# Rewriting the order of work at the end of an attention phase: last softmax first, smaller norm groups

## The reference, cut to what matters

```python
def _L3_gnn_ref(H, W_lin, W_val, a, W_out, A0, src, dst):
    Xq = (H @ W_lin.T).reshape(bt, n, h, dh)
    Xv = (H @ W_val.T).reshape(bt, n, h, dh)
    e = jnp.einsum('behd,hd->beh', jax.nn.leaky_relu(Xq[:, src] + Xq[:, dst], 0.2), a)
    e = e + jnp.log(A0[src, dst] + EPS)[None, :, None]
    e_t = e.transpose(1, 0, 2)
    m = jax.ops.segment_max(e_t, src, num_segments=n)
    ex = jnp.exp(e_t - m[src])
    attn = ex / jax.ops.segment_sum(ex, src, num_segments=n)[src]
    Y = jax.ops.segment_sum(attn[..., None] * Vt, src, num_segments=n)
    return Y.transpose(1, 0, 2, 3).reshape(bt, n, d) @ W_out.T

x = _layernorm(x + _L3_gnn_ref(x, ...), axis=-1)      # (x - mean) / sqrt(var + 1e-5)
```

## Time and profile before

| | |
|---|---|
| median of 3 runs | 995.13 us (993.33 to 995.75) |
| the profiled execution's own time | 996.82 us |
| its span in the trace | 994.9 us |
| mean granted PE clock | 0.983 of full speed |
| PE / DVE / ACT / POOL busy, share of the span | 94% / 67% / 55% / 31% |

### The profile page before, as it was taken

How to read it: one execution, slowest core, us unless ns; L and a number is a source line. 1 busy time by engine, 2 the same in 40 slices (tenths; PEclk the granted TensorE clock), 3 DMA queues, 4 the chain that set the end, 5 groups by cost and what they waited for, 6 DMA issues and landing times. The chain is left out here.

```text
span 994.9 us, 14572 instructions
## 1 busy us (share of the span) xinstructions
PE 933.1 (94%) x5202; PEld 801.6 (81%) x5202; DVE 664.6 (67%) x1628; ACT 546.2 (55%) x1136; POOL 311.3 (31%) x289
## 2 busy tenths in 40 slices
PE   7999998999999999999999999899989999978993
PEld 5689987899998898998889899788778974556773
DVE  7665444445647657665755775598887877788867
ACT  2042314764636565554656564557677648475667
POOL 3011222331233234223323333224333230155663
PEclk9999999999999999999999999999999999999998
DMA  8040011001010100101010010301010000000014
GB/s 227 2 82 22 2 43 64 22 22 43 1 44 1 43 22 1 43 2 43 1 43 22 3 42 1 125 1 56 14 39 22 1 1 1 0 1 1 1 43 127
DMA packets 33994, 31.62 MB, mean 32 GB/s; under 512 B 8450, under 2 KB 28034, under 8 KB 33924
## 3 DMA queue, kind: packets, MB, share of 16 engines
q1 hardware_dynamic: 32900, 30.64, 10.0%
q10 hardware_dynamic: 960, 0.07, 0.1%
q0 software_dynamic: 64, 0.00, 0.0%
HBM read 22.83 MB, written 7.87 MB: 31 GB/s over the span
## 5 line engine op out<-in xcount | busy, mean ns | idle before, releaser
L1368 ACT ACTIVATE gates<-psum,gbias 128x256 f32<-128x256 f32 (+2 forms) x312 | 159.2, 565 | 70.5 <-PE psum L67 66.1
L65 PE MATMUL psum<-LS,WI 128*128 128x256 f32 (+2 forms) x312 | 104.1, 334 | 8.8 <-ACT gates L1368 6.2
L78 POOL TENSOR_TENSOR LS<-A,LS 128x512 fp32r<-128x512 f32 (+2 forms) x44 | 48.6, 1105 | 177.5 <-ACT LS L1353 177.4
L67 PE MATMUL psum<-LS,WI 128*128 128x256 f32 (+2 forms) x312 | 102.9, 330 | 0.0
L66 PE MATMUL psum<-LS,WI 128*128 128x256 f32 (+2 forms) x312 | 102.9, 330 | 0.0
L78 POOL TENSOR_TENSOR LS<-Hodd,LS 128x512 fp32r<-128x512 f32 (+2 forms) x44 | 48.3, 1097 | 153.2 <-ACT LS L1353 153.2
L78 DVE TENSOR_TENSOR yl<-psum,yh 128x512 fp32r<-128x512 f32 x58 | 39.6, 689 | 65.5 <-ACT yh L1310 43.9
L78 POOL TENSOR_TENSOR XSl<-X,XSh 128x512 fp32r<-128x512 f32 x32 | 43.0, 1344 | 107.0 <-ACT XSh L1305 107.0
L65 PE MATMUL psum<-B2h,LT2h 128*128 128x256 f32 x256 | 72.7, 284 | 1.0 <-DVE X L1481 1.0
L65 PEld LDWEIGHTS psum<-LS,WI 128*128 128x128 f32 x312 | 59.2, 190 | 17.4 <-POOL LS L78 10.2
L67 PE MATMUL psum<-B2h,LT2l 128*128 128x256 f32 x256 | 72.4, 283 | 0.0
(11 more groups left out here) (379 smaller groups left out, 2699.8 us busy)
## 6 DMA issues: line engine op xcount, KB each, us to landing
WI<-lstm_weights SPq DMA_DIRECT2D x14, 512.0 KB, 3.6
WH<-lstm_weights SPq DMA_DIRECT2D x11, 512.0 KB, 4.6
X<-in_x SPq DMA_DIRECT2D x16, 256.0 KB
out<-X SPq DMA_DIRECT2D x16, 256.0 KB, 2.3
lstm_weights<-WI SPq DMA_DIRECT2D x4, 512.0 KB, 3.2
lstm_weights<-WH SPq DMA_DIRECT2D x3, 512.0 KB, 2.7
A<-in_adj SPq DMA_DIRECT2D x4, 256.0 KB, 4.4
z_A<-in_adj SPq DMA_DIRECT2D x1, 1024.0 KB, 5.3
```

What stands on the lines that cost most here:

```text
L65: pe.matmul(out, lhs[0], rhs[0], start=start, stop=False)
L67: return pe.matmul(out, lhs[1], rhs[0], start=False, stop=stop)
L78: return eng.tensor_tensor(out, full, high.bitcast(F32), ALU.subtract)
L1368: act.activation(gates[:, gate, 0:n], sh.psum[:, gate, 0:n], ACT.Tanh if gate == G else ACT.Sigmoid, bias=gbias[:, p_ - 1, gate:gate + 1]) ...
```

## The change

`GROUPS4` is cut into eight groups instead of seven: (0,4), then pairs (4,6), (6,8), (8,10), (10,12), (12,14), and 14 and 15 alone. `drain()` is written out from ("vh", 8) and ("U", 15) on, earlier than before, and two slots fewer are generated ahead of it. No instruction is dropped, and only the variance, power and shift of one more group are added. In `drain()`'s new order

- `W` 14 stands ahead of `S` 7 and `W` 15 ahead of `S` 8;
- `sc`, `mx`, `df` of the last softmax stand right behind `R` 6, ahead of `s4` 6 and of any variance;
- on GpSimd `va` 12 and `va` 13 stand ahead of `p4` 1, and `va` 14 and 15 ahead of `p4` 2;
- on ACT `ap4` 0 comes behind `vh` 8, `U` 15, `S` 7 and `vh` 9; `ap4` 1, 2 and 3 are spread behind `vh` 13, `vh` 14 and `S` 14; `ap4` 4 to 15 come behind `S` 15.

```diff
-        GROUPS4 = [(0, 4), (4, 7), (7, 9), (9, 11), (11, 13), (13, 15), (15, 16)]
+        GROUPS4 = [(0, 4)] + [(b, b + 2) for b in range(4, NB - 2, 2)] + [(NB - 2, NB - 1), (NB - 1, NB)]
@@ drain() @@
-            first = [("vh", 10), ("sc", 3), ("mx", 3), ("df", 3), ("S", 9), ("vl", 10), ("ex", 3), ("va", 11), ("S", 10),
-                     ("R", 7), ("at", 3), ("vh", 11), ("ec", 3), ("vl", 11), ("p4", 1), ("dn", 3), ("va", 12), ("ap4", 3)]
-            weighted = [("P", 8), ("P", 9), ("s4", 7), ("R", 8), ("sh4", 1), ("ap4", 4), ("vh", 12), ("S", 11), ("R", 9), ("vl", 12),
-                        ("va", 13), ("s4", 8), ("v4", 2), ("P", 10), ("p4", 2), ("S", 12), ("vh", 13), ("s4", 9), ("R", 10),
-                        ("vl", 13), ("va", 14), ("ap4", 5), ("P", 11), ("S", 13), ("vh", 14), ("s4", 10), ("R", 11),
-                        ("vl", 14), ("va", 15), ("v4", 3), ("p4", 3), ("P", 12), ("sh4", 2), ("ap4", 6), ("S", 14),
-                        ("vh", 15), ("s4", 11), ("R", 12), ("vl", 15)]
-            last = [("P", 13), ("ap4", 7), ("S", 15), ("s4", 12), ("v4", 4), ("p4", 4), ("R", 13), ("sh4", 3), ("ap4", 8),
-                    ("P", 14), ("s4", 13), ("ap4", 9), ("R", 14), ("P", 15), ("s4", 14), ("v4", 5), ("p4", 5), ("sh4", 4),
-                    ("R", 15), ("ap4", 10), ("s4", 15), ("v4", 6), ("p4", 6), ("ap4", 11), ("ap4", 12), ("sh4", 5),
-                    ("ap4", 13), ("ap4", 14), ("sh4", 6), ("ap4", 15)]
-            return first + weighted + last
+            softmax = [("vh", 8), ("U", 15), ("lr", 14), ("W", 14), ("R", 5), ("vl", 8), ("S", 7), ("s4", 5), ("lr", 15), ("P", 6),
+                       ("va", 9), ("W", 15), ("vh", 9), ("ap4", 0), ("R", 6), ("sc", 3), ("vl", 9), ("S", 8), ("va", 10), ("mx", 3),
+                       ("df", 3), ("vh", 10), ("vl", 10), ("ex", 3), ("S", 9), ("va", 11), ("at", 3), ("v4", 1), ("ec", 3), ("vh", 11),
+                       ("vl", 11), ("s4", 6), ("dn", 3), ("va", 12), ("va", 13)]
+            weighted = [("P", 7), ("S", 10), ("P", 8), ("R", 7), ("vh", 12), ("S", 11), ("s4", 7), ("p4", 1), ("vl", 12), ("vh", 13),
+                        ("v4", 2), ("R", 8), ("P", 9), ("ap4", 1), ("va", 14), ("S", 12), ("vl", 13), ("s4", 8), ("R", 9), ("va", 15),
+                        ("vh", 14), ("S", 13), ("p4", 2), ("P", 10), ("s4", 9), ("vl", 14), ("ap4", 2), ("R", 10), ("vh", 15), ("S", 14),
+                        ("sh4", 1), ("v4", 3), ("vl", 15), ("p4", 3), ("P", 11), ("ap4", 3), ("s4", 10), ("S", 15), ("sh4", 2), ("ap4", 4),
+                        ("ap4", 5)]
+            last = [("P", 12), ("R", 11), ("ap4", 6), ("s4", 11), ("v4", 4), ("p4", 4), ("R", 12), ("sh4", 3), ("P", 13), ("ap4", 7),
+                    ("s4", 12), ("R", 13), ("P", 14), ("ap4", 8), ("s4", 13), ("v4", 5), ("p4", 5), ("R", 14), ("ap4", 9), ("P", 15),
+                    ("sh4", 4), ("s4", 14), ("v4", 6), ("p4", 6), ("ap4", 10), ("R", 15), ("ap4", 11), ("s4", 15), ("v4", 7), ("p4", 7), ("sh4", 5),
+                    ("ap4", 12), ("ap4", 13), ("sh4", 6), ("ap4", 14), ("sh4", 7), ("ap4", 15)]
+            return softmax + weighted + last
@@ order @@
-        for k_ in range(NB + 2):
+        for k_ in range(NB):
```

## The result

The changed kernel takes 998.29 us (median of 8 runs, 995.67 to 999.03), the kernel before 995.1 us (8 runs, 993.33 to 996.34). The ratio on record is 1.0025, 95% interval 1.0015 to 1.0035: 2.5 us slower (the two medians themselves lie 3.2 us apart, inside the same interval). That is within the 0.3% that I had called no change, but clear of the noise, and past my likeliest +0.7 us.

A forecast was written before the change was run, and what follows sets the result against it. ACT's backlog was taken to bound the end: idle 8.5 against 7.4 us gave +1.1, the walk's end against the trace's +0.4, against the old order's walk +0.7. From median 995.13 that made 995.8 us, range 993.6 to 998.1.

The forecast's parts named there:

- the 0.3% that I had called no change: Whole time: only 0.3% (3.0 us) can be told from no change; faster 0.04, same 0.90, slower 0.06.
- my likeliest +0.7 us: Whole kernel: ACT ends 0.7 us later than in the old order walked with the same prices; spread +0.4 to +1.1, chance 0.58.
- ACT's walk: ACT from 953.96 to its end: in the new order idle sums to 8.5 us against 7.4, ending at about 992.1.
- rival C: PE's pause from 961.5 on: its clock falls, losing at most 1.75 us more, +2.5 in all, 997.6 us; chance 0.20.
- the range's end: Whole time: the forecast's upper limit, 998.1 us, the clock-fall case with a little of the runs' spread.
- DVE ahead of `ec`: Between `at` and `dn`: `dn` 0.58 us after `at`; the added group's variances and shift about 0.75 us on DVE, hidden.
- the end of ACT is its work plus its idle time: Last 41 us: ACT's work stays the same, so the change wins only what it takes from 7.4 us of idle time.
- 12 ready blocks lay unused ahead of S 10: ACT's 3.0 us gap ahead of S 10: none of `ap4` 1 to 3, 4.7 us of ready work, is put there.
- rival B: Kernel end: it follows PE, so P 15 being 3.7 to 4.2 us earlier shows in full, 991.4 us; chance 0.04.
- the eighth group costs nothing: Norm groups: one more costs DVE about 0.75 us and GpSimd's powers 10.3 instead of 9.9, both hidden behind ACT.

The follow-up runs named there:

- run 1: The changed kernel plus nine PE matmuls nobody reads, five between S 9 and `at` 3, four between `at` 3 and `dn` 3: ratio 0.9995 to the kernel before.
- run 5: The changed kernel with `ec` 3 ahead of `v4` 1 and five unread matmuls, four ahead of `at` 3, one ahead of `dn` 3: ratio 0.9988 to the kernel before.
- run 9: The kernel before with only `W` 14 ahead of S 7, `W` 15 ahead of S 8, and `sc`, `mx`, `df` 3 ahead of `s4` 6: ratio 0.9998.
- run 2: The changed kernel with one swap on DVE, `ec` 3 ahead of `v4` 1: ratio 1.0006 to the kernel before.
- run 3: The changed kernel with `ap4` 1, 2 and 3 (12 blocks) moved ahead of S 10 on ACT: ratio 1.0017 to the kernel before.
- run 7: The changed kernel's order with the kernel before's seven norm groups, and `v4` 1 behind `ec` 3: ratio 1.0013 to the kernel before.
- run 10: The changed kernel with its whole end reordered, 24 blocks behind S 15, and no unread matmuls: ratio 0.9955 to the kernel before, 990.3 us.
- run 11: The changed kernel plus five unread PE matmuls between S 9 and `at` 3 only: ratio 1.0000 to the kernel before.

## Why the prediction was right or wrong, point by point

- **Right in its places, half right in its size: ACT's walk.** It put gaps of 2.7, 0.9, 0.8, 3.0 and 1.1 us ahead of `vh` 8, S 7, `ex`, S 10 and S 11; with the clock kept up (run 1) they are 2.59, 0.97, 0.38 (and 0.45 behind it), 3.05 and 0.92. The 40 blocks behind S 15, the end in ACT, and no wait for a shift are in the trace as said. `ex` came 7.0 us after `aT` instead of 9.5: the softmax is 2.5 us earlier, 2.4 were forecast. But the +0.7 us hides two errors. The walk's conditions (full clock, hardly a queue ahead of `ec`) are those of run 5, which measures 36.3 us and no loss at all, where the walk had 36.7 for the new order and 36.0 for the old. And the queue that it left out costs 0.7 to 0.8 us. Together they made run 1's +0.8 look like a hit, which is luck.
- **Wrong: which case is the likeliest.** I gave the fall of PE's clock, rival C, 0.20 and left it out of the forecast. It happened, where it was put (between `dn` 3 and S 11), and its price, bounded at 1.75 us, measured 1.7: +0.7 + 1.75 was 997.6 us, and 995.1 times 1.0025 is 997.6; that this fits so well is luck in part, since its +0.7 stood for something else. The step that failed is the weighing of the two rows: I held 1.69 busy of 3.0 us without a fall against 1.46 with one and gave the new pause, 1.2 by my own walk, the benefit of the doubt, though it was below both (the trace has 1.57 of the 3 us from 961 on and 1.21 of those from 959.8 on). Nor could that row have settled it: in run 9 PE is busy 1.41 of 3.0 us, less than the 1.46, and the clock stays up. The median itself, 998.29, lies 0.2 us above the range's end; the part ahead of the change adds its own spread to that.
- **Mis-sized: DVE ahead of `ec`.** The walk put `dn` 0.58 us after `at`, as in the kernel before, and costed a whole group's variances and shift at 0.75 us, hidden; beside GpSimd the five variances alone took 1.53, and `dn` came 1.20 us after `at`. That is 0.6 us late in the trace; undoing it gave 0.7 (run 2) and 0.8 (run 5 against run 1). I had thought of that stretching for the softmax's scans only. So the 2.5 us are 1.7 of clock and 0.7 to 0.8 of queue, and without both the stretch comes out even (run 5).
- **Wrong in its reason: "the end of ACT is its work plus its idle time".** As a sum that is always true, and it forecast well because ACT was busy without a gap over 0.15 us behind S 11's copy. As an explanation it fell in run 3: filling the gap only made others. What can't move is S 15's copy and what is written behind it. My complaint that 12 ready blocks lay unused ahead of S 10 was right as an observation and worth 0.3 us.
- **Right: rival B (the end follows PE) is out.** PE's last products did come earlier: in the changed kernel S 15's copy starts 22.7 us after `aT`, against 26.4, and P 15, by an estimate from rows that hold several batches, 25.1 us after it against 27.1 (with the clock kept up, run 1, 23.6; the walk had 22.9). It bought nothing, since the tail grew from 9.4 to 15.6 us: 26.4 + 0.5 + 9.4 = 36.3, 22.7 + 0.5 + 15.6 = 38.8. By these two sums the result can be read at a glance. The Trainium skill's goal of keeping the matmul engine busy (Perfetto Trace Analysis, "Optimization Strategies") would have picked the change; the measurement decides against it in this stretch.
- **Right: the eighth group costs nothing** (run 7). What I had not seen is that it gives 0.7 us at S 14, by taking `v4` 2 off the path of `vl` 14.

What stays open is what makes the clock fall. The runs show that in the changed kernel's order the first pause decides, and neither a pause's length nor a busy share sorts the cases: a pause of 0.88 us ahead of `at` 3 came with a fall (changed kernel, run 2), one of 0.92 us at the same place without (run 10); PE busy 1.83 of 3 us came with a fall (run 2), 1.69 and even 1.41 of 3 (run 9, the row below) without. Each of these is one traced execution; whether the clock falls in every execution of a kernel is not shown. Nor is it known why the part ahead of the attention phase differs by up to 2.7 us between executions.

```profile
967.00:970.00 3.00, 1.41 (x10) 1.17 (x10) 1.58 (x6) 2.43 (x6) 1.25 (x4) 1.00 0.11 31
```

## What to carry to other kernels

At the end of a kernel, find the last item that can't start earlier and count what each engine has written behind it: time saved ahead of that item is given back block by block if ready work is moved behind it, and ready work moved from one gap to another wins nothing. When a change makes a busy TensorE pause, put the half clock into the forecast as a term with a price of its own, even where pauses as long went unpunished elsewhere, and test it with a few matmuls that nobody needs. A small copy on which another engine waits belongs ahead of work that only a later stage wants.

## What the hardware showed that I had not expected

Nine matmuls without use (some 2.1 us of PE) made this stretch 1.7 us shorter, and five of them 1.9 us (run 11). A DVE instruction on 128x8 elements, 0.17 us elsewhere, took 0.68 us beside GpSimd's `vl` (the five instructions of a variance took 1.53 us instead of the 0.65 of 972.75 to 973.40 in the kernel before). The Trainium skill, GPSIMD Engine Reference, "Key points", says that GpSimd shares its SBUF interfaces with VectorE and contends with instructions that have two inputs in SBUF; the trace agrees for the variance's first, third and fourth instruction, 0.68, 0.37 and 0.32 us, and doesn't show it for the second, 0.15 us, which has two such inputs as well.
